# Scattering normalised rows to the experts' slots: from DRAM in the routing stage, or from SBUF in the experts' stage

## The chip, the cores and the metric

The kernel runs on one core of a Trainium2 chip as one launch. The core has a tensor engine (PE, with its weight loads shown apart as PEld), a vector engine (DVE), a scalar engine (ACT), GpSimd (POOL) and a sync engine (SP) that issues most DMAs. The metric is the device time of the launch in microseconds; a version's time is the median of its runs.

## The reference, cut to what matters

Two layers run over x of 8 batches of 256 tokens, 256 wide, each layer an attention and a feed-forward, each with a residual. The place that matters is the first layer's end and the mixture of eight experts behind it:

```python
x = x + _L0_xattn_ref(_layernorm(x, axis=-1), ctx_1024, ...)   # two attentions, then relu(x @ Wf1 + bf1) @ Wf2 + bf2
x = x + _L0_ffn_ref(_layernorm(x, axis=-1), gate_w, W1, W2, W3)

def _L0_ffn_ref(x, gate_w, W1, W2, W3):
    xf = x.reshape(-1, D)
    scores = xf @ gate_w.T
    expert_weights, expert_indices = jax.lax.top_k(scores, 2)
    expert_weights = jax.nn.softmax(expert_weights, axis=-1)
    mid = jax.nn.silu(einsum('td,ehd->teh', xf, W1)) * einsum('td,ehd->teh', xf, W3)
    out_all = jnp.einsum('teh,edh->ted', mid, W2)
    ...   # the two chosen experts' rows, weighted and summed
```

Every token needs two of the eight experts only. The kernel therefore sorts the 2 x 2048 (token, expert) pairs by expert into `xs`, a DRAM tensor of 23 tiles of 256 rows, in which each tile belongs to one expert, and computes tile by tile.

## The kernel before

The program is a chain of stages: `decoder` (both attentions), `feed_forward`, `route`, `experts`, `memory_attention`, `mixture`. Each stage is one block with a queue of instructions written out by hand for each engine; the order in a queue is the order of the code, semaphores tie the queues together, and at a block's end every engine drains its pipeline and all five meet in a barrier before the next block starts.

- `feed_forward` goes batch by batch. Its last steps normalise the result (DVE, L1542, into the ring `res_n`), turn it on PE (`turn_result`, L1451) for the gate's scores (`gates`, L1460; `logits`, L1555), and store two things from SP's queue: the result itself to `xa` (L1400) and the normalised rows to the DRAM tensor `hm` (L1403), 256 KB for each batch. SP also clears `xs` with zeros (L1393), and waits at the block's end until the stores have landed (L1408).
- `route` finds each pair's slot. SP loads `hm` back into `route_rows` (L1656, eight loads). DVE finds the top two, counts them, adds up the counts, and writes `slots` (L1748, once for each of the two choices k) and at last `tile_expert`, the expert of each tile (L1752 to L1757). POOL waits for the rows, the zeros and each choice's slots, and then issues 32 indirect DMAs (L1775), each of which writes 128 rows of 1 KB to their slots in `xs`; it waits at the end until all have landed.
- `experts` goes over the 23 tiles as a pipeline. For a tile, SP reads its expert's number from `tile_expert` and loads its rows `x_in` (L1841), its up weights `up_in` (L1844, 1792 KB) and its down weights `down_in` (L1836, 896 KB), all in rings of two. ACT and DVE split each into a high and a low half in 16 bits: `up_hl` HI on ACT (L1929), LO on DVE (`up_low`, L1956), seven pieces each. PE turns the rows (`turn_rows`, L1867) into `ps_x`; ACT (L1934) and DVE (L1984) split those into `x_hl`. Then PE multiplies up (`go_up`, L1880) and, two steps later in its queue, down (`go_down`, L1892). At step t PE does go_up(t+1), turn_rows(t+2), go_down(t); SP issues down_in(t+2), x_in(t+3), up_in(t+3) and stores y(t-1).

Of the kernel before, what the change touches and what calls it, by code (L numbers as in the profile page):

```python
# [14 lines left out]
P = 128  # L15
BATCHES = 8
SEQ = 256
TOKENS = BATCHES * SEQ
D = 256
# [1305 lines left out]
def feed_forward(nc, c, rows, x, w1_hl, b1, w2_hl, b2, gain, shift, gate, out, out_normed, logits, xs, zeroed):  # L1325


    with ExitStack() as ctx:
# [28 lines left out]
        res_n = ring(sb, "res_n", [P, TT, D])  # L1357
# [19 lines left out]
        res_stored, res_n_stored = ring(sem, "res_stored"), ring(sem, "res_n_stored")  # L1377
# [4 lines left out]
        with nc.Block() as block:  # L1382
            @block.sync
            def _(sp):
# [5 lines left out]
                def step(t):  # L1390
                    old, older = t.plus(-2), t.plus(-4)
# [13 lines left out]
                pipeline(sp, step, 0, 4)  # L1405
                for k in range(2):
                    sp.wait_ge(res_stored[k], 16 * (BATCHES // 2))
                    sp.wait_ge(res_n_stored[k], 16 * (BATCHES // 2))  # L1408

            @block.tensor  # L1410
            def _(pe):
# [33 lines left out]
                def turn_result(t):  # L1445
# [3 lines left out]
                    for k in range(TT):  # L1449
                        for dc in range(DC):  # L1450
                            mm = nc.tensor.transpose(ps_r[:, dc, k * P:(k + 1) * P], res_n[t.slot][:, k, dc * P:(dc + 1) * P], c.ident[:, :])  # L1451
# [58 lines left out]
            def _(dve):  # L1510
# [10 lines left out]
                def step(t):  # L1521
# [94 lines left out]
def route(nc, c, logits, normed, xs, weights, slots, tile_expert, zeroed):  # L1616
# [6 lines left out]
    with ExitStack() as ctx:  # L1623
# [21 lines left out]
        rows = sb("rows", [P, NT, D])  # L1645
# [4 lines left out]
        gap_done, slots_done, rows_loaded, scattered = sem("gap_done"), sem("slots_done"), sem("rows_loaded"), sem("scattered")  # L1650

        with nc.Block() as block:
            @block.sync
            def _(sp):
                for b in range(BATCHES):
                    sp.dma_start(rows[:, b * TT:(b + 1) * TT, :], normed[b]).then_inc(rows_loaded, 16)  # L1656

# [102 lines left out]
            def _(pool):  # L1760
# [9 lines left out]
                pool.wait_ge(rows_loaded, 16 * BATCHES)  # L1770
                pool.wait_ge(zeroed, 16 * BATCHES)
# [697 lines left out]
```

## Time and profile before

| | us |
|---|---|
| median of 3 runs | 1415.44 (1414.83 to 1420.32) |
| the profiled execution, its own time | 1417.55 |
| its span in the trace | 1415.8 |
| feed_forward's end and route, up to tile_expert | about 500 to 524.2 in the span |
| the scatter and its end | 523.0 to 567.7 |
| the head of experts, up to the first go_up | 567.7 to 585.6 |
| the 23 tiles of experts | 585.6 to about 957 |

The profile is of one execution. Times in its rows are from the start of the span. A timeline row is the start, the duration, the engine, the line of the kernel, the operation, output and inputs, and in brackets how long the engine was idle before and what released it. PEclk is the clock that PE was granted, as a share of 2.4 GHz (0.50 is 1.2 GHz). DMA is the mean busy share of the core's 16 DMA engines.

### The profile page before, as it was taken

How to read it: one execution, taken by the hardware profiler on the slowest of the kernel's cores; microseconds unless marked ns; L12 is line 12 of the kernel's file. 1: busy time of each engine (PE TensorE's matmuls, PEld its weight loads, DVE VectorE, ACT ScalarE, POOL GpSimd, SP SyncE). 2: the span in 40 equal slices, each digit the busy share in tenths (PEclk: the TensorE clock that was granted, in tenths of full speed). 3: DMA queues.
4: the chain of work that ended last, by engine and by line, in shares of the span. 5: the costliest groups of instructions: out<-in, count | busy, mean ns of one | idle time of the engine just before them, and what ended most of it. 6: DMA issues, size and time to landing. Idle time of an engine off the chain costs nothing. (4 is left out here: it accounts for less than half of the span.)

```text
span 1415.8 us, 26094 instructions
## 1 busy us (share of the span) xinstructions
PE 1086.1 (77%) x9362; PEld 734.0 (52%) x9362; DVE 944.0 (67%) x2608; ACT 610.6 (43%) x1227; POOL 431.5 (30%) x595
## 2 busy tenths in 40 slices
PE   2788888888399820388999999991577874999998
PEld 1465544444178720277778777881234432554554
DVE  4748777776247640478888888871677752677676
ACT  2346666666255300455666666641266661000000
POOL 4235764333426637012211121116543100010010
PEclk9978889998699955699999999995599996999999
DMA  6423335231123232656666666515332211000000
GB/s 182 125 83 106 99 95 158 80 91 46 34 78 119 103 108 100 231 206 231 243 218 208 236 241 222 199 44 170 103 90 75 80 38 61 31 30 23 31 8 16
DMA packets 127397, 164.26 MB, mean 116 GB/s; under 512 B 13075, under 2 KB 106022, under 8 KB 124326
## 3 DMA queue, kind: packets, MB, share of 16 engines
q1 hardware_dynamic: 123686, 153.41, 33.2%
q0 software_dynamic: 3584, 9.18, 2.0%
q8 instruction: 76, 1.25, 0.4%
q14 instruction: 51, 0.42, 0.1%
HBM read 117.01 MB, written 45.35 MB: 115 GB/s over the span
## 5 line engine op out<-in xcount | busy, mean ns | idle before, releaser
L1880 PE MATMUL moe_ps_u<-moe_x_hl,moe_up_hl 128*128 128x256 f16 x1932 | 227.5, 277 | 41.4 <-DVE moe_up_hl L1956 33.2
L1880 PEld LDWEIGHTS moe_ps_u<-moe_x_hl,moe_up_hl 128*128 128x128 f16 x1932 | 185.3, 99 | 83.6 <-DVE moe_up_hl L1956 39.7
L2129 PE MATMUL mix_ps_e<-wr_hl,mix_u_hl 128*128 128x512 f16 x768 | 173.4, 382 | 0.0
L2006 POOL CAST moe_mid_hl<-moe_mid 128x256 f16<-128x256 f32 x161 | 68.5, 425 | 315.5 <-DVE moe_mid L1971 315.5
L547 ACT ACTIVATE dec_probs<-dec_ps_t 128x768 f32<-128x768 f32 (+1 forms) x128 | 117.2, 916 | 77.5 <-PE dec_ps_t L449 76.5
L1956 DVE SCALAR_TENSOR_TENSOR moe_up_hl<-moe_up_in,moe_up_hl 128x512 f16<-128x512 f32 x161 | 105.2, 687 | 55.9 <-ACT moe_up_hl L1929 55.9
L2241 DVE SCALAR_TENSOR_TENSOR mix_acc<-mix_ps_e,mix_shares,mix_acc 128x256 f32<-128x256 f32 x256 | 110.4, 478 | 39.7 <-PE mix_ps_e L2129 39.3
L1929 ACT ACTIVATE moe_up_hl<-moe_up_in 128x512 f16<-128x512 f32 x161 | 99.1, 619 | 63.5 <-DMA moe_up_in<-in_moe_w 63.5
L2129 PEld LDWEIGHTS mix_ps_e<-wr_hl,mix_u_hl 128*128 128x128 f16 x768 | 75.1, 98 | 84.1 <-issue 2.4
L645 DVE CUSTOM_DVE_ANT_0 dec_dropped<-dec_ps_s,mask_row 128x128 bf16<-128x128 f32 (+1 forms) x256 | 76.1, 353 | 49.8 <-PE dec_ps_s L436 49.3
L1892 PE MATMUL moe_ps_y<-moe_down_hl,moe_mid_hl 128*128 128x256 f16 x966 | 109.0, 273 | 0.0
L649 DVE TENSOR_REDUCE dec_neg_m<-dec_ps_s 128x2 f32<-128x512 f32 x128 | 82.5, 687 | 36.1 <-PE dec_ps_s L436 36.1
L1971 DVE SCALAR_TENSOR_TENSOR moe_mid<-moe_ps_u,moe_mid 128x256 f32<-128x256 f32 x161 | 66.9, 415 | 52.5 <-ACT moe_mid L1924 52.4
L1892 PEld LDWEIGHTS moe_ps_y<-moe_down_hl,moe_mid_hl 128*128 128x128 f16 x966 | 94.6, 98 | 10.7
L1197 DVE TENSOR_REDUCE mem_neg_m<-mem_ps_s 128x2 f32<-128x512 f32 x128 | 82.3, 685 | 26.5 <-PE mem_ps_s L1041 25.8
L436 PE MATMUL dec_ps_s<-dec_k_st,dec_q_st 48*128 48x256 f16 (+1 forms) x512 | 53.7, 291 | 55.4 <-DMA dec_k_st<-dec_k_dram 36.0
L1963 DVE TENSOR_TENSOR moe_mid_hl<-moe_mid,moe_mid_hl 128x256 f16<-128x256 f32 x161 | 92.1, 583 | 0.0
L1924 ACT ACTIVATE moe_mid<-moe_ps_u 128x256 f32<-128x256 f32 x161 | 61.7, 383 | 66.3 <-PE moe_ps_u L1880 59.4
L1125 ACT ACTIVATE mem_probs<-mem_ps_t 128x1024 f32<-128x1024 f32 x64 | 65.4, 1024 | 39.3 <-PE mem_ps_t L1052 39.1
L481 PE MATMUL dec_ps_far<-dec_probs,dec_v 128*32 128x256 f32 (+1 forms) x1024 | 68.9, 391 | 2.4 <-DVE dec_att L658 1.1
L436 PEld LDWEIGHTS dec_ps_s<-dec_k_st,dec_q_st 48*128 48x128 f16 x512 | 17.3, 97 | 94.7 <-DMA dec_k_st<-dec_k_dram 40.0
L1974 DVE SCALAR_TENSOR_TENSOR moe_down_hl<-moe_down_in,moe_down_hl 128x256 f16<-128x256 f32 x161 | 66.2, 411 | 0.0
(275 smaller groups left out, 1965.6 us busy)
## 6 DMA issues: line engine op xcount, KB each, us to landing
moe_up_in<-in_moe_w SPq DMA_DIRECT2D x23, 1792.0 KB, 7.5
moe_down_in<-in_moe_w SPq DMA_DIRECT2D x23, 896.0 KB, 4.6
dec_q_dram<-dec_q_hl SPq DMA_DIRECT2D x48, 128.0 KB, 1.9
dec_k_dram<-dec_k_hl SPq DMA_DIRECT2D x48, 128.0 KB, 1.9
dec_q_st<-dec_q_dram SPq DMA_DIRECT2D x64, 96.0 KB, 2.6
dec_k_st<-dec_k_dram SPq DMA_DIRECT2D x64, 96.0 KB, 2.7
xs<-zeros SPq DMA_DIRECT2D x8, 736.0 KB
moe_x_in<-xs SPq DMA_DIRECT2D x23, 256.0 KB, 4.3
```

The source lines that it names most:

```text
L436: return nc.tensor.matmul(ps_s[h % 2][:, k, 0:keys_of(n, k)], q_st[n % 2][at:at + STACK, pair, k * P:(k + 1) * P], k_st[n % 2][at:at + STA ...
L547: nc.scalar.activation(probs[p % 4][:, :, 0:w], ps_t[p % 2][:, :, 0:w], ACT.Exp, scale=SCALE).then_inc(exps_done, 1)
L645: ins = nc.vector.tensor_tensor_reduce(dropped[h % 2][:, k, 0:w], ps_s[h % 2][:, k, 0:w], c.mask_row[:, SEQ - w:SEQ], -1.0, -MASKED, ALU.a ...
L649: nc.vector.tensor_reduce(neg_m[n % 2][:, :, column(h):column(h) + 1], ps_s[h % 2][:, :, :], AX.X, ALU.max, negate=True).then_inc(max_done, 1)
L1197: nc.vector.tensor_reduce(neg_m[n % 2][:, :, column(h):column(h) + 1], ps_s[h % 2][:, :, :], AX.X, ALU.max, negate=True).then_inc(max_done, 1)
L1880: mm = nc.tensor.matmul(bank[:, m, :], up_hl[t.slot][:, w, m, dc, f * P:(f + 1) * P], x_hl[t.slot][:, x, dc, :], start=(dc == 0 and w == x ...
L1892: mm = nc.tensor.matmul(ps_y[t.slot][:, k, :], mid_hl[t.slot][:, m, f, k * P:(k + 1) * P], down_hl[t.slot][:, w, f, :], start=(f == 0 and ...
L1929: nc.scalar.activation(up_hl[new.slot][:, HI, :, :, f * P:(f + 1) * P].rearrange("p m c h -> p (m c) h"), up_in[new.slot][:, :, :, f * P:( ...
L1956: nc.vector.scalar_tensor_tensor(up_hl[t.slot][:, LO, :, :, at].rearrange("p m c h -> p (m c) h"), up_in[t.slot][:, :, :, at].rearrange("p ...
L1963: nc.vector.tensor_tensor(mid_hl[t.slot][:, LO, f, :], mid[:, f, :], mid_hl[t.slot][:, HI, f, :], ALU.subtract).then_inc(mid_split, 1)
L2129: mm = nc.tensor.matmul(ps_e[fill % RING][:, :, :], u_hl[t.slot][:, r, dc, k * P:(k + 1) * P], wr_hl[:, m, dc, 2 * q:2 * q + 2, :], start= ...
L2241: nc.vector.scalar_tensor_tensor(acc[t.slot][:, k, :], ps_e[(TT * q + k) % RING][:, j, :], shares[t.slot][:, k, 2 * q + j:2 * q + j + 1], ...
```

## The change

The normalised rows get an SBUF tensor of their own for all batches, `normed_rows`, which lives until the end. `feed_forward` writes them there and turns them from there; the ring `res_n`, the tensor `hm`, its eight stores and its eight loads are gone, and so are DVE's two waits before a slot of `res_n` is written again. The 32 indirect DMAs and their wait for the zeros move from POOL's queue in `route` to the head of POOL's queue in `experts`; nothing in `route` waits for them. In `experts` SP issues the first tile's up and down weights and the second's up weights, and only then waits for the scatter and loads the first tile's rows. Of the later tiles SP loads the rows right behind the down weights, one step later than before. For the first tile DVE does all seven `up_low` ahead of the low half of the rows.

```diff
@@ feed_forward
-        res_n = ring(sb, "res_n", [P, TT, D])
@@ sync
-                    if older.within():
-                        sp.wait_ge(res_n_done, TT * (older.n + 1))
-                        sp.dma_start(out_normed[older.n], res_n[older.slot][:, :, :]).then_inc(res_n_stored[older.slot], 16)
@@ vector
-                        if d.before(2):
-                            dve.wait_ge(res_n_stored[d.slot], 16 * d.turn)
-                            dve.wait_ge(r_turned, d.n - 1)
                         for k in range(TT):
-                            nc.vector.tensor_scalar(res_n[d.slot][:, k, :], res[d.slot][:, k, :], mv_o[d.slot][:, k, 0:1],
+                            nc.vector.tensor_scalar(normed_rows[:, d.n * TT + k, :], res[d.slot][:, k, :], mv_o[d.slot][:, k, 0:1],
@@ route
-            @block.sync
-            def _(sp):
-                for b in range(BATCHES):
-                    sp.dma_start(rows[:, b * TT:(b + 1) * TT, :], normed[b]).then_inc(rows_loaded, 16)
@@ gpsimd
-                pool.wait_ge(rows_loaded, 16 * BATCHES)
-                pool.wait_ge(zeroed, 16 * BATCHES)
-                for k in range(2):
-                    pool.wait_ge(slots_done, k + 1)
-                    for t in range(NT):
-                        nc.gpsimd.indirect_dma_start(xs[:, :], bass.IndirectOffsetOnAxis(ap=slots[:, k, t:t + 1], axis=0),
-                                                     rows[:, t, :], None).then_inc(scattered, 16)
-                pool.wait_ge(scattered, 16 * 2 * NT)
@@ experts, sync
+                def load_rows(t):
+                    if t.n == 0:
+                        sp.wait_ge(scattered, 16 * 2 * NT)
+                    if t.before(2):
+                        sp.wait_ge(turned, t.n - 1)
+                    sp.dma_start(x_in[t.slot][:, :, :], xs_t[t.n]).then_inc(x_loaded[t.slot], 16)
+
                 def step(t):
                     new, ahead, old = t.plus(2), t.plus(3), t.plus(-1)
+                    if t.n == -1:
+                        load_rows(t.plus(1))
                     if new.within():
 ...
                         sp.dma_start(down_in[new.slot][:, :, :], w2[e]).then_inc(down_loaded[new.slot], 16)
+                    if new.within() and new.n > 0:
+                        load_rows(new)
                     if ahead.within():
                         e = sp.value_load(tile_expert[0:1, bass.ds(ahead.n, 1)], min_val=0, max_val=E - 1)
-                        if ahead.before(2):
-                            sp.wait_ge(turned, ahead.n - 1)
-                        sp.dma_start(x_in[ahead.slot][:, :, :], xs_t[ahead.n]).then_inc(x_loaded[ahead.slot], 16)
@@ vector
+                    if new.n == 0:
+                        for f in range(0, HC, 2):
+                            up_low(new, f)
                     if new.within():
                         dve.wait_ge(x_hi, new.n + 1)
 ...
                     for f in range(0, HC, 2):
-                        if new.within():
+                        if new.within() and new.n > 0:
                             up_low(new, f)
@@ gpsimd
+                pool.wait_ge(zeroed, 16 * BATCHES)
+                for k in range(2):
+                    for t in range(NT):
+                        nc.gpsimd.indirect_dma_start(xs[:, :], bass.IndirectOffsetOnAxis(ap=slots[:, k, t:t + 1], axis=0),
+                                                     rows[:, t, :], None).then_inc(scattered, 16)
```

POOL's queue from the end of `route` to the first tile of `experts`, before; an unconditional branch is the end of a block or the start of the next, and `barrier` stands for the meeting of the five engines:

```order
L1768 AFFINE_SELECT route_triangle<-route_triangle 128x128 [waits route_made]
L1775 DMA xs<-route_rows,slots 5888x256 [waits route_slots_done,zeroed,route_rows_loaded]
L1775 DMA xs<-route_rows,slots 5888x256 x15
L1775 DMA xs<-route_rows,slots 5888x256 [waits route_slots_done]
L1775 DMA xs<-route_rows,slots 5888x256 x15
L1652 UNCONDITIONAL_BRANCH [waits route_scattered]
L1998 UNCONDITIONAL_BRANCH [waits barrier_Pool_Activation_PE_DVE_SP_gather]
L2006 CAST moe_mid_hl0<-moe_mid 128x256 [waits moe_mid_done] x7
```

Here all 32 indirect DMAs and the wait for their landing are behind `slots` and ahead of the barrier. The same place on POOL now:

```order
L1754 AFFINE_SELECT route_triangle<-route_triangle 128x128 [waits route_made]
L1643 UNCONDITIONAL_BRANCH
L1989 UNCONDITIONAL_BRANCH [waits barrier_Pool_Activation_PE_DVE_SP_gather]
L1994 DMA xs<-normed_rows,slots 5888x256 [waits zeroed]
L1994 DMA xs<-normed_rows,slots 5888x256 x31
L2003 CAST moe_mid_hl0<-moe_mid 128x256 [waits moe_mid_done] x7
```

The scatter has gone from ahead of the barrier to behind it, and the wait for its landing has left POOL.

SP's queue at the head of `experts`, before (0 and 1 behind a name are the slots of a ring):

```order
L1828 UNCONDITIONAL_BRANCH [waits barrier_Pool_Activation_PE_DVE_SP_release]
L1838 TENSOR_LOAD tile_expert
L1838 ISA x2
L1841 DMA moe_x_in0<-xs 128x2x256
L1844 ISA
L1844 DMA moe_up_in0<-in_moe_w13 128x3584
L1833 TENSOR_LOAD tile_expert
L1833 ISA x2
L1836 ISA
L1836 DMA moe_down_in0<-in_moe_w2 128x1792
```

Here the first tile's rows are the first DMA behind the barrier. SP's queue now, from the first load of weights on:

```order
L1832 DMA moe_up_in0<-in_moe_w13 128x3584
L1822 TENSOR_LOAD tile_expert
L1822 ISA x2
L1825 ISA
L1825 DMA moe_down_in0<-in_moe_w2 128x1792
L1829 TENSOR_LOAD tile_expert
L1829 ISA x2
L1832 ISA
L1832 DMA moe_up_in1<-in_moe_w13 128x3584
L1815 DMA moe_x_in0<-xs 128x2x256 [waits moe_scattered]
```

The first tile's rows, which stood first, now stand behind three loads of weights, with the wait for the scatter; the second tile's down weights, its rows and the third tile's up weights follow.

DVE's queue at the head of `experts`, before (`up_hl` are the halves of the up weights, `x_hl` those of the rows):

```order
L1951 UNCONDITIONAL_BRANCH [waits barrier_Pool_Activation_PE_DVE_SP_release]
L1956 SCALAR_TENSOR_TENSOR moe_up_hl0<-moe_up_in0,moe_up_hl0 128x4x128 [waits moe_up_hi] x3
L1984 TENSOR_TENSOR moe_x_hl0<-moe_ps_x,moe_x_hl0 128x512 [waits moe_x_hi]
L1956 SCALAR_TENSOR_TENSOR moe_up_hl0<-moe_up_in0,moe_up_hl0 128x4x128 [waits moe_up_hi] x4
L1971 SCALAR_TENSOR_TENSOR moe_mid<-moe_ps_u0,moe_mid 128x256 [waits moe_silu_done]
```

Here the rows' low half stands between three and four pieces of the weights. The same place on DVE now:

```order
L1939 UNCONDITIONAL_BRANCH [waits barrier_Pool_Activation_PE_DVE_SP_release]
L1944 SCALAR_TENSOR_TENSOR moe_up_hl0<-moe_up_in0,moe_up_hl0 128x4x128 [waits moe_up_hi] x7
L1975 TENSOR_TENSOR moe_x_hl0<-moe_ps_x,moe_x_hl0 128x512 [waits moe_x_hi]
L1959 SCALAR_TENSOR_TENSOR moe_mid<-moe_ps_u0,moe_mid 128x256 [waits moe_silu_done]
L1962 SCALAR_TENSOR_TENSOR moe_down_hl0<-moe_down_in0,moe_down_hl0 128x256 [waits moe_down_hi]
```

All seven pieces of the first tile's weights now stand ahead of the rows; of later tiles nothing moved on DVE.

## Rows read from the trace of the kernel before

**Rows 1.** Stretches: busy us of PE, PEld, DVE, ACT, POOL; PEclk; DMA; GB/s.

```profile
524.50:568.70 44.20, 0.00 (x0) 0.00 (x0) 0.00 (x0) 0.00 (x0) 29.76 (x31) 0.50 0.23 95
568.70:585.60 16.90, 1.11 (x4) 0.71 (x4) 5.17 (x8) 4.22 (x8) 0.00 (x0) 0.50 0.93 366
```

**Rows 2.** Timeline of the scatter: its first, second and last indirect DMA.

```profile
522.93 0.41 DVE L1752 TENSOR_TENSOR route_ended<-route_ends,route_tile_numbers 1x184 f32<-1x184 f32 x1
522.97 1.24 POOL L1775 DMA_INDIRECT xs<-route_rows,slots  x1 [11.17 <-DVE slots L1748]
...
524.52 0.96 POOL L1775 DMA_INDIRECT xs<-route_rows,slots  x1 [0.30 <-issue]
...
562.46 0.96 POOL L1775 DMA_INDIRECT xs<-route_rows,slots  x1 [0.30 <-issue]
```

**Rows 3.** The end of route's block: duration ns min/median/max, first and last start.

```profile
L1652 DVEq DRAIN  x1: 448/448/448, 523.8 to 523.8; - x1
...
L1652 POOLq COMPARE_BRANCH  x1: 33/33/33, 564.9 to 564.9; - x1
L1652 POOLq DRAIN  x1: 2675/2675/2675, 565.0 to 565.0; - x1
```

**Rows 4.** Tensor xs, 522 to 568: issue to landing of the scatter's DMAs.

```profile
DMA to landing us min/median/max: 2.4/2.4/2.7
```

**Rows 5.** Timeline of the head of experts.

```profile
568.75 0.37 SPq L1841 DMA_DIRECT2D moe_x_in<-xs  x1
...
571.40 1.11 PE L1867 MATMUL moe_ps_x<-ident,moe_x_in 128*128 128x128 f32 x4 [54.66 <-DMA moe_x_in<-xs]
...
581.86 0.56 ACT L1934 CAST moe_x_hl<-moe_ps_x 128x512 f16<-128x512 f32 x1
582.46 0.69 DVE L1984 TENSOR_TENSOR moe_x_hl<-moe_ps_x,moe_x_hl 128x512 f16<-128x512 f32 x1 [0.30 <-ACT moe_x_hl L1934]
...
585.61 12.53 PE L1880 MATMUL moe_ps_u<-moe_x_hl,moe_up_hl 128*128 128x256 f16 x84 [13.10 <-DVE moe_up_hl L1956]
```

**Rows 6.** A later block's start: POOL's barrier event, then POOL's first gather.

```profile
L98 POOLq EVENT_SEMAPHORE  x4: 17/17/17, 378.3 to 960.2; - x4
...
961.05 1.01 POOL L1292 DMA_INDIRECT mem_y<-ys,slots  x1 [12.29 <-POOLq L98]
```

**Rows 7.** Stretch with eight gathers beside loads from SP, columns as rows 1.

```profile
962.00:970.00 8.00, 0.00 (x0) 0.00 (x0) 0.00 (x0) 0.00 (x0) 5.87 (x8) 0.50 1.06 359
```

**Rows 8.** An indirect DMA beside DVE (timeline); the head's `up_low` (groups by line).

```profile
995.01 0.73 DVE L1245 TENSOR_SCALAR mem_h_rows<-mem_sums,mem_mv,mem_rstd 128x256 f32<-128x256 f32 x2
995.18 1.12 POOL L1277 DMA_INDIRECT mem_kv_rows<-table,mem_best_row  x1 [5.95 <-DVE mem_best_row L1217]
...
L1956 DVE SCALAR_TENSOR_TENSOR moe_up_hl<-moe_up_in,moe_up_hl 128x512 f16<-128x512 f32 x7 | 4.6, 687 | 55.9 <-ACT moe_up_hl L1929 55.9
```

**Rows 9.** DMA issues on the page: count, KB each, us to landing.

```profile
moe_up_in<-in_moe_w SPq DMA_DIRECT2D x23, 1792.0 KB, 7.5
moe_down_in<-in_moe_w SPq DMA_DIRECT2D x23, 896.0 KB, 4.6
```

**Rows 10.** Waits of SP, then of POOL, and feed_forward's last drain on PE.

```profile
SPq L1408 <- DMA hm<-ff_res_n: 3.6, 1, 3.6
...
POOL xs L1775 <- DVE slots L1748: 11.2, 1, 11.2
...
L1382 PEldq DRAIN  x1: 1902/1902/1902, 508.4 to 508.4; - x1
```

**Rows 11.** Steady state of experts: a tile; landing of down_in, then of x_in.

```profile
871.21 0.34 SPq L1836 DMA_DIRECT2D moe_down_in<-in_moe_w  x1
...
884.81 0.60 PE L1867 MATMUL moe_ps_x<-ident,moe_x_in 128*128 128x128 f32 x4
...
DMA to landing us min/median/max: 4.4/4.6/14.1
...
DMA to landing us min/median/max: 2.6/4.3/13.7
```

More of the change, by code:

```diff
@@ L1322, in _, with feed_forward @@
                         add_outputs(mixed)
-def feed_forward(nc, c, rows, x, w1_hl, b1, w2_hl, b2, gain, shift, gate, out, out_normed, logits, xs, zeroed):
+def feed_forward(nc, c, rows, x, w1_hl, b1, w2_hl, b2, gain, shift, gate, out, normed_rows, logits, xs, zeroed):
     with ExitStack() as ctx:
@@ L1390, in step @@
                 def step(t):
-                    old, older = t.plus(-2), t.plus(-4)
+                    old = t.plus(-2)
                     if t.within():
@@ L1400, in step @@
                         sp.dma_start(out[old.n], res[old.slot][:, :, :]).then_inc(res_stored[old.slot], 16)
-                    if older.within():
-                        sp.wait_ge(res_n_done, TT * (older.n + 1))
-                        sp.dma_start(out_normed[older.n], res_n[older.slot][:, :, :]).then_inc(res_n_stored[older.slot], 16)
-                pipeline(sp, step, 0, 4)
+                pipeline(sp, step, 0, 2)
                 for k in range(2):
                     sp.wait_ge(res_stored[k], 16 * (BATCHES // 2))
-                    sp.wait_ge(res_n_stored[k], 16 * (BATCHES // 2))
             @block.tensor
@@ L1613, in _, with route @@
                 pipeline(pool, step, 1, 2)
-def route(nc, c, logits, normed, xs, weights, slots, tile_expert, zeroed):
+def route(nc, c, logits, weights, slots, tile_expert):
     with ExitStack() as ctx:
@@ L1644, in route @@
         gap, exped, both = sb("gap", [P, NT]), sb("exped", [P, NT]), sb("both", [P, NT])
-        rows = sb("rows", [P, NT, D])
         ps_p = ctx.enter_context(nc.psum_tensor("route_ps_p", [P, BANK], F32))
@@ L1769, in _, with experts @@
                                         pattern=[[1, P]], channel_multiplier=-1).then_inc(made, 1)
-                pool.wait_ge(rows_loaded, 16 * BATCHES)
-                pool.wait_ge(zeroed, 16 * BATCHES)
-                for k in range(2):
-                    pool.wait_ge(slots_done, k + 1)
-                    for t in range(NT):
-                        nc.gpsimd.indirect_dma_start(xs[:, :], bass.IndirectOffsetOnAxis(ap=slots[:, k, t:t + 1], axis=0),
-                                                     rows[:, t, :], None).then_inc(scattered, 16)
-                pool.wait_ge(scattered, 16 * 2 * NT)
-def experts(nc, c, xs, w13, w2, tile_expert, ys, matrices):
+def experts(nc, c, rows, slots, xs, zeroed, w13, w2, tile_expert, ys, matrices):
     with ExitStack() as ctx:
@@ L1800, in experts @@
         E, HC = w2.shape[0], w2.shape[2]
+        NT = slots.shape[2]
         x_in, x_hl = ring(sb, "x_in", [P, TT, D]), ring(sb, "x_hl", [P, 2, DC, SEQ], F16)
@@ L1808, in experts @@
         ps_y = ring(ps, "ps_y", [P, TT, D])
+        scattered = sem("scattered")
         x_loaded, up_loaded, down_loaded = ring(sem, "x_loaded"), ring(sem, "up_loaded"), ring(sem, "down_loaded")
@@ L2379, in program @@
         ctx_hl = dram("ctx_hl", [2, D, TOKENS], F16)
-        xa, hm = dram("xa", rows), dram("hm", rows)
+        xa = dram("xa", rows)
+        normed_rows = sb("normed_rows", [P, BATCHES * TT, D])
         logits = sb("logits", [P, BATCHES * TT, E])
@@ L2393, in program @@
             feed_forward(nc, c, resident, i["x"], w1_hl, i["bf1"], w2_hl, i["L0_xattn_bf2"], i["L0_xattn_g3"], i["L0_xattn_be3"],
-                         i["gate"], xa, hm, logits, xs, zeroed)
-        route(nc, c, logits, hm, xs, shares, slots, tile_expert, zeroed)
+                         i["gate"], xa, normed_rows, logits, xs, zeroed)
+        route(nc, c, logits, shares, slots, tile_expert)
         wc_hl, ws_hl, cent_hl = parts(ctx, "wc_hl", [D]), parts(ctx, "ws_hl", [D]), parts(ctx, "cent_hl", [routed])
         wr_hl = parts(ctx, "wr_hl", [routed, D])
-        experts(nc, c, xs, i["moe_w13"], i["moe_w2"], tile_expert, ys,
+        experts(nc, c, normed_rows, slots, xs, zeroed, i["moe_w13"], i["moe_w2"], tile_expert, ys,
                 [([i["mem_wc"]], flat(wc_hl)), ([i["centroids"]], flat(cent_hl)), ([i["mix_ws"][0], i["mix_ws"][1]], flat(ws_hl)),
```

6 lines of the change are left out of this document (3 added, 3 removed).

## The prediction, made before the result

> **What bounds the kernel now.** I read the page's forty slices first. PE's digits fall to 0 in one place only, a good third of the way in; that is the place of the change, and the busy shares of the whole span say nothing about it. The stretches cut at that place show why [rows 1]: from 524.5 to 568.7 no engine but POOL works, and the DMA engines are 23% busy at 95 GB/s; from 568.7 to 585.6 the opposite, POOL idle and the DMA engines 93% busy at 366 GB/s. Two pieces of work that use different things stand one behind the other.
>
> The timeline gives the chain through that gap. The scatter's first indirect DMA starts at 522.97 and its last at 562.46 [rows 2]; from the second on they follow every (562.46 - 524.52) / 30 = 1.265 us, 0.96 of work and 0.30 of issue. Each lands 2.4 after its start [rows 4]. The view of the block's end then tells what a look at the timeline alone would hide: POOL's wait for the landings is over at 564.9, but its drain takes another 2.68, to 567.7, and only then does the barrier open [rows 3]. SP reads the expert's number and issues the first tile's rows at 568.75; PE turns them from 571.40; and the first `go_up` starts at 585.61, released by DVE's last piece of the up weights [rows 5]. So the end of the gap hangs on weights that were asked for only after the scatter had ended. From 585.61 the 23 tiles run, and everything later hangs on them: what moves that start moves the end by as much.
>
> **The change part by part.** The sum is the time of the first `go_up`, against the profiled execution (1417.55, span 1415.8).
>
> *Stores and loads of the normalised rows: 0.* The eight stores: SP waits 3.6 for the last of them at the block's end, but PE's drain there, from 508.4 for 1.90, ends at 510.3, after it [rows 10]. If PE were quicker, the cover would be gone and up to 3.6 could be won; it isn't. The eight loads: what released POOL's first scatter was DVE's `slots`, after a wait of 11.2 [rows 10]; the rows were there. In SP's queue nothing on the path stood behind either. The two waits taken from DVE released nothing in the trace.
>
> *The scatter starts later: +2.2.* It now waits not for the first choice's slots but for the block's end: DVE's last drain ends at 523.8 + 0.45 = 524.25 [rows 3]. From there to POOL's first indirect DMA I take 0.95: at a later block start it came 0.85 after POOL's barrier event [rows 6], and from POOL's drain (567.7) to SP's first DMA, a register load included, it was 1.05 [rows 3, 5]. That is 525.2 against 522.97. Bounds 1.9 to 2.6.
>
> *The scatter itself: +1.7, bounds -0.3 to +4.5.* 31 steps of 1.265 are 39.2, against 39.5 before, since the first took 1.24 instead of 0.96, with DVE instructions beside it [rows 2]: -0.3. New is what runs beside it: SP's loads, and seven `up_low` of 0.687 on DVE [rows 8]. The loads I cost at nothing: eight gathers keep their step (8 starts in 8 us, 5.87 busy as far as they are counted there) while the DMA engines are saturated at 359 GB/s [rows 7]. For DVE two rows give a price: the first scatter, beside an instruction with two SBUF inputs, was 0.28 longer, and a gather beside a DVE instruction on SBUF took 1.12, 0.16 longer [rows 2, 8]. Nothing for a DVE instruction is the lower end, its whole 0.687 the upper. I take 0.28, the row with two SBUF inputs as `up_low` has them: 7 x 0.28 = 2.0; the ends are 0 and 4.8.
>
> *The end of the scatter: -3.75.* SP now waits for the landings itself, and issues the rows some 0.1 after. Before, 564.9 to 568.75 = 3.85 went to POOL's drain, the barrier and SP's register load [rows 3, 5]. All three are now over long before: POOL's drain in `route` stands behind nothing but a select, and SP has done its register loads beside the scatter.
>
> *The weights leave the path: -11.7.* From SP's issue of the rows to PE is 2.65, and from PE to `go_up` was 14.21 [rows 5]. Of that only the rows' own steps remain: 1.11 on PE, 0.56 on ACT, 0.69 on DVE, and three hand-overs of some 0.05, together 2.5 [rows 5]. What hides the rest is the scatter: up, down and the next up are 4480 KB [rows 9], at 366 GB/s [rows 1] 12.5 us from about 525; with the scatter's traffic beside them they are there by 541, and the conversions, under 5 us of ACT and DVE [rows 8], end by 546. The rows come at about 571: 25 us of cover. Without it the 11.7 would be back on the path. All seven `up_low` being ahead of the rows' low half in DVE's queue matters here; before, four of them stood behind it.
>
> *SP's queue behind the new wait.* The second tile's down weights, its rows and the third tile's up weights stand behind it. They are issued by about 570, where before they went at 573 to 586; who waits for them is ACT and PE some 12 us after `go_up` begins, against landings of 4.3 to 7.5 [rows 9, 11]: 0. POOL is free again at 568, before the first cast is asked for.
>
> *Rows of later tiles one step later: 0.* In the steady state x_in now goes right behind down_in, issued at 871.21, and PE turns those rows at 884.81 [rows 11]: with 0.4 for the issue, 13.2 of slack against a median landing of 4.3.
>
> Sum: +2.2 - 0.3 + 2.0 - 3.75 - 11.7 = -11.5. The profiled execution would take 1406.0; it was 2.1 above the median, and the median would be 1415.4 - 11.5 = **1403.9**. With DVE's price at 0 it is 1401.9, at its upper end 1406.7; a first x_in that lands at its median instead of 2.65 adds 1.7.
>
> PE's clock enters on neither side: it is at its lower level all through the gap [rows 1] and will be at the new start.
>
> **A port that is locked (rival 1).** Every `up_low` could hold POOL's descriptor work for its whole length, 7 x 0.687 = 4.8 instead of 2.0: 1406.7. Against it: the first scatter overlapped three DVE instructions and lost 0.28 in all. The Trainium skill says so much (SBUF — State Buffer, section SBUF: two separate sides): DVE and GpSimd share a pair of ports, which the first comer holds for its whole instruction; a DVE instruction with two SBUF inputs shuts out a GpSimd instruction that reads SBUF. By that rule this rival is the time; the trace bears out a delay, but no full one.
>
> **Loads that push the scatter out (rival 2).** If POOL could not write descriptors while the weights' 12.5 us of transfer fill the queues, the scatter would lose that much: 1403.9 + 12.5 = 1416.4 at the most, no change. Against it stand the eight gathers at full step [rows 7], though they are gathers, and eight.
>
> **Rows that come too late (rival 3, slower).** If x_in behind down_in in every tile took longer than its slack of 13.2, PE would wait in each of 21 tiles. The point from which it makes the kernel slower is 13.2 + 11.5 / 21 = 13.75. At down_in's longest landing, 14.1 [rows 11], it costs 21 x 0.9 = 18.9: 1422.8. For it: x_in's longest landing is 13.7, and down_in now stands ahead of it. Against: the median is 4.3, and up_in goes out 3 us after it, as before.
>
> **Not beside (rival 4).** If the weights were held with the scatter all the same, only the drain and the barrier would be saved, and the start lost: 1415.4 + 2.2 - 3.75 = 1413.9. SP's order, three loads ahead of the wait, speaks against it.
>
> **How the numbers follow.** Forecast 0.76, rival 1 0.09, rival 2 0.07, rival 3 0.04, rival 4 0.04. Half a per cent is 7.1 us, about what a measurement of this kernel can tell from no change: below 1408.4 is faster, and that holds the forecast and rival 1, 0.85; rivals 2 and 4 are the same, 0.11; rival 3 slower, 0.04. The range goes from 1400 (no price on DVE, and the shortest ends of the start) to 1409 (rival 1 with a slow first x_in); rivals 2 to 4, 0.15, are left out.
>
> **What would show it.** Right: weights of the first tile issued at about 525, before most of the scatter; indirect DMAs starting near 525.2 in steps of 1.265, a few longer where `up_low` runs; x_in of the first tile issued 2.5 after the last start, near 569; `go_up` near 574 with the rows' low half as its releaser, no longer `up_low`. Steps that stay long in the whole first 15 us would mean rival 2, PE waiting for x_in in later tiles rival 3. The forecast is wrong if the scatter takes over 46 us.

## The result, and the profile after

| | before | after |
|---|---|---|
| median, us (runs) | 1415.52 (7) | 1403.40 (7) |
| lowest to highest, us | 1407.11 to 1420.32 | 1400.95 to 1408.88 |
| profiled execution, us | 1417.55 | 1402.28 |
| its span, us | 1415.8 | 1400.5 |

The medians are 12.1 us apart. The ratio of the two kernels over their runs is 0.9921, with a 95% interval of 0.9894 to 0.9947: the change is faster, by 7.5 to 15 us as far as the whole time can tell. The prediction was 1403.9 us, in a range of 1400 to 1409.

The gap in which POOL worked alone is still there, but the weights are now inside it. Three stretches of that gap in the changed kernel show this (busy us of PE, PEld, DVE, ACT, POOL; the granted clock; DMA share; GB/s):

```profile
520.00:530.00 10.00, 0.00 (x0) 0.00 (x0) 1.31 (x6) 0.00 (x0) 5.95 (x6) 0.50 0.62 221
530.00:541.00 11.00, 0.00 (x0) 0.00 (x0) 4.50 (x7) 3.75 (x7) 8.56 (x9) 0.50 0.89 368
541.00:565.00 24.00, 0.00 (x0) 0.00 (x0) 0.00 (x0) 0.00 (x0) 17.75 (x19) 0.50 0.29 103
```

In [rows 1] one stretch had 95 GB/s and a busy POOL, the next 366 GB/s and an idle POOL. Now 530 to 541 has 368 GB/s, a busy POOL, and DVE's and ACT's work on the first weights. PE's clock is at its lower level in all of them, as before. The timeline of the changed kernel gives the head of the new stage:

```profile
519.52 0.17 DVE L1734 CAST slots<-route_slot 128x16 int32<-128x16 f32 x1
...
521.32 0.16 DVE L1743 TENSOR_SCALAR tile_expert<-route_owner 1x23 int32<-1x23 f32 x1
522.52 1.24 POOL L1994 DMA_INDIRECT xs<-normed_rows,slots  x1 [13.08 <-POOLq L1643]
522.75 0.36 SPq L1832 DMA_DIRECT2D moe_up_in<-in_moe_w  x1
523.91 0.35 SPq L1825 DMA_DIRECT2D moe_down_in<-in_moe_w  x1
...
525.04 0.34 SPq L1832 DMA_DIRECT2D moe_up_in<-in_moe_w  x1
```

The scatter now starts 3.00 us behind the first `slots` (it was 1.10), released by the barrier of line 1643; SP's three weight loads go out between its first steps. The end of the scatter, and the way to the first `go_up`, in the same timeline:

```profile
563.27 0.96 POOL L1994 DMA_INDIRECT xs<-normed_rows,slots  x1 [0.30 <-issue]
565.70 0.39 SPq L1815 DMA_DIRECT2D moe_x_in<-xs  x1
...
568.41 0.34 SPq L1832 DMA_DIRECT2D moe_up_in<-in_moe_w  x1
...
568.50 1.11 PE L1855 MATMUL moe_ps_x<-ident,moe_x_in 128*128 128x128 f32 x4 [54.12 <-DMA moe_x_in<-xs]
569.65 0.59 ACT L1922 CAST moe_x_hl<-moe_ps_x 128x512 f16<-128x512 f32 x1 [35.41 <-PE moe_ps_x L1855]
570.27 0.69 DVE L1975 TENSOR_TENSOR moe_x_hl<-moe_ps_x,moe_x_hl 128x512 f16<-128x512 f32 x1 [33.42 <-ACT moe_x_hl L1922]
...
571.11 1.22 PE L1868 MATMUL moe_ps_u<-moe_x_hl,moe_up_hl 128*128 128x256 f16 x5 [1.49 <-DVE moe_x_hl L1975]
```

Against [rows 5], `go_up` is now released by the rows' low half, and no longer by the weights'. From the last indirect DMA to x_in it takes 2.43, in place of 6.29.

All kernels below are compared by the same five times, each between two marks of a profiled execution: the decoder's end (POOL's event of line 98, [rows 6]), the first `slots`, the first `go_up`, and the experts' end (the second such event). "Way" is from `slots` to `go_up`, the stretch the prediction was about.

| kernel | decoder | to `slots` | way | tiles | the rest | span |
|---|---|---|---|---|---|---|
| before | 378.3 | 143.6 | 63.74 | 374.6 | 455.6 | 1415.8 |
| after | 375.7 | 143.8 | 51.59 | 373.7 | 455.7 | 1400.5 |
| e1_rows_only | 376.2 | 143.8 | 62.07 | 373.7 | 462.0 | 1417.8 |
| e2_head_no_overlap | 377.4 | 145.2 | 60.44 | 374.5 | 459.2 | 1416.7 |
| e3_rows_by_dram | 373.8 | 143.6 | 51.51 | 373.6 | 454.9 | 1397.4 |
| e4_low_halves_behind | 379.8 | 143.5 | 52.88 | 374.6 | 460.0 | 1410.8 |
| e5a_two_inputs | 373.7 | 142.4 | 50.26 | 374.4 | 457.1 | 1397.9 |
| e5b_one_input | 382.9 | 145.9 | 50.43 | 374.4 | 462.9 | 1416.5 |
| e6_after_again | 378.8 | 144.2 | 51.57 | 373.6 | 458.4 | 1406.6 |
| e7_second_tile_too | 380.0 | 143.5 | 51.05 | 369.9 | 458.9 | 1403.3 |

The way is 12.15 us shorter after the change, and repeats there: 51.59, 51.57 and, with the rows sent through DRAM, 51.51. The kernel before was profiled once, and e1 and e2 show below that 1.4 to 1.7 of its 63.74 are a slow landing of the first weights. The decoder runs the same code in all ten and still takes 373.7 to 382.9; the rest takes 454.9 to 462.9. So of the 15.3 us between the two profiled spans, 2.6 in the decoder are not the change's. The part on PE's clock, at the end of the experiments, says what goes with these two columns.

### The profile page after: what moved, and what is told of

It reads as the page before. It is cut to its first block and busy times, and to the rows that moved or that the text cites. A ratio compares the mean times of both kernels' runs of the same rounds, so it can differ in the third digit from the quotient of the medians.

```text
span 1400.5 us, 26069 instructions
## 1 busy us (share of the span) xinstructions
PE 1075.2 (77%) x9362; PEld 730.0 (52%) x9362; DVE 942.8 (67%) x2608; ACT 611.0 (44%) x1227; POOL 432.3 (31%) x595
## 3 DMA queue, kind: packets, MB, share of 16 engines
HBM read 114.91 MB, written 43.25 MB: 113 GB/s over the span
```

## Experiments

**Which part of the change brings the time?** Theory A: the overlap of scatter and weight loads, and the drain of POOL that leaves the path. Rival B: less traffic, since the rows stay in SBUF.

**e1_rows_only**, rows kept, scatter left in `route` (against the kernel before):

```diff
-                        sp.wait_ge(res_n_done, TT * (older.n + 1))
-                        sp.dma_start(out_normed[older.n], res_n[older.slot][:, :, :]).then_inc(res_n_stored[older.slot], 16)
...
-                            nc.vector.tensor_scalar(res_n[d.slot][:, k, :], res[d.slot][:, k, :], mv_o[d.slot][:, k, 0:1],
+                            nc.vector.tensor_scalar(normed_rows[:, d.n * TT + k, :], res[d.slot][:, k, :], mv_o[d.slot][:, k, 0:1],
...
-                for b in range(BATCHES):
-                    sp.dma_start(rows[:, b * TT:(b + 1) * TT, :], normed[b]).then_inc(rows_loaded, 16)
...
-                pool.wait_ge(rows_loaded, 16 * BATCHES)
```

> The kernel before with one part of the change: the normalised rows stay in SBUF (eight stores, eight loads and their waits are gone), and the scatter stays at the end of the route, with the barrier behind it. Theory A (the gain is the overlap of scatter and weight loads): the stores and loads were hidden, so the time is that of the kernel before, 1415.5 us within 1.5 us, and from the scatter's last DMA_INDIRECT to the first go_up matmul it stays near 21.5 us. Rival B (the gain is the 2.1 MB less written and 2.1 MB less read): near 1403.4 us.

Measured: 1418.97 us, ratio 1.0032 (1.0010 to 1.0055) to the kernel before. No gain; B falls. The timeline of e1_rows_only shows the path of before:

```profile
521.08 1.24 POOL L1760 DMA_INDIRECT xs<-normed_rows,slots  x1 [11.15 <-DVE slots L1734]
...
521.85 0.43 DVE L1743 TENSOR_SCALAR tile_expert<-route_owner 1x23 int32<-1x23 f32 x1
...
560.56 0.96 POOL L1760 DMA_INDIRECT xs<-normed_rows,slots  x1 [0.30 <-issue]
566.89 0.37 SPq L1826 DMA_DIRECT2D moe_x_in<-xs  x1
567.48 0.36 SPq L1829 DMA_DIRECT2D moe_up_in<-in_moe_w  x1
...
574.66 3.75 ACT L1914 ACTIVATE moe_up_hl<-moe_up_in 128x512 f16<-128x512 f32 x7 [61.88 <-DMA moe_up_in<-in_moe_w]
...
582.07 1.67 PE L1865 MATMUL moe_ps_u<-moe_x_hl,moe_up_hl 128*128 128x256 f16 x7 [11.35 <-DVE moe_up_hl L1941]
```

From the last indirect DMA to x_in again 6.33, and `go_up` waits for the weights. The way is 62.07; the 1.7 us against 63.74 lie in the first up weights, which came 7.2 after their issue here (567.48 to 574.66) and 8.9 after it in the profile of before:

```profile
569.34 0.36 SPq L1844 DMA_DIRECT2D moe_up_in<-in_moe_w  x1
...
578.21 3.75 ACT L1929 ACTIVATE moe_up_hl<-moe_up_in 128x512 f16<-128x512 f32 x7 [63.55 <-DMA moe_up_in<-in_moe_w]
```

That the median is 4 us above before (1414.77 in the 28 runs beside it) was not expected: 1.5 us was the bound. In this profile it stands neither in the way nor in the tiles but in the rest, 462.0. About half of it goes with PE's granted clock, averaged over each run: the runs of before are 3.8 us shorter for each 0.01 more of it (a straight line through the 28, correlation -0.71), and e1's ten were granted 0.8847 on average, against 0.8905. Where the other 2 us come from is not shown.

**e2_head_no_overlap**, the scatter in its new place, SP's and DVE's order of before (against the changed kernel; SP's part, DVE's is the edit of e4 below):

```diff
-                    if t.n == -1:
-                        load_rows(t.plus(1))
...
-                    if new.within() and new.n > 0:
-                        load_rows(new)
...
+                        if ahead.n == 0:
+                            sp.wait_ge(scattered, 16 * 2 * NT)
+                        if ahead.before(2):
+                            sp.wait_ge(turned, ahead.n - 1)
+                        sp.dma_start(x_in[ahead.slot][:, :, :], xs_t[ahead.n]).then_inc(x_loaded[ahead.slot], 16)
```

> The changed kernel, but SyncE's and VectorE's order in the experts' stage is that of the kernel before: the scatter stands at the head of the experts' stage, x_in of tile 0 with its wait for the scatter is SyncE's first transfer, and all weights are issued behind it. Theory A: the scatter starts 1.9 us later, the drain of GpSimd and the barrier behind it go (3.75 us), and the weights stay on the path: near 1413.6 us, so a sixth of the gain. Rival B (the place of the scatter alone, or the residence of the rows, brings it): near 1403.4 us.

Measured: 1414.97 us, ratio 1.0001 (0.9979 to 1.0022). No gain that can be told from none, and far from 1403.4: the new place alone does not do it. The timeline of e2_head_no_overlap has both small terms:

```profile
522.56 0.17 DVE L1734 CAST slots<-route_slot 128x16 int32<-128x16 f32 x1
...
525.56 1.24 POOL L1985 DMA_INDIRECT xs<-normed_rows,slots  x1 [13.08 <-POOLq L1643]
...
565.14 0.96 POOL L1985 DMA_INDIRECT xs<-normed_rows,slots  x1 [0.31 <-issue]
567.57 0.37 SPq L1823 DMA_DIRECT2D moe_x_in<-xs  x1
```

The start is 3.00 behind `slots` (1.9 later than before), x_in 2.43 behind the last indirect DMA (3.86 earlier), together -2.0; the way fell to 60.44, of which 1.4 is again the weights' quicker landing. From 60.44 to 51.59 only the order of SP and DVE differs: 8.9 us are what this order brings in this pair of profiles, what the scatter loses beside DVE already taken off.

**e3_rows_by_dram**, the overlap with the rows sent through DRAM as before (against the changed kernel; the eight stores and the ring `res_n`, not shown here, are back as well):

```diff
+                for b in range(BATCHES):
+                    sp.dma_start(rows[:, b * TT:(b + 1) * TT, :], normed[b]).then_inc(rows_loaded, 16)
...
+                pool.wait_ge(rows_loaded, 16 * BATCHES)
                 pool.wait_ge(zeroed, 16 * BATCHES)
```

> The changed kernel, but with the rows sent through DRAM again (eight stores in the feed-forward, eight loads in the route into the same SBUF tensor, the scatter waits for them too); the overlap of scatter and weight loads stays. Theory A: same time as the changed kernel, 1403.4 us within 1.5 us, since stores and loads lie beside other work. Rival B (residence): near 1415.5 us. Between the two ends the distance from 1403.4 us is what the residence itself is worth.

Measured: 1400.61 us, ratio 0.9913 (0.9880 to 0.9946), the same as the changed kernel within the intervals (2.8 us below it, where 1.5 was expected), at 117.01 MB read in place of 114.91. The way is 51.51 and the stretch to `slots` 143.6, in place of 51.59 and 143.8. So between these marks the residence is worth nothing in time, and the medians, which can tell these two kernels apart to some 6 us, show nothing either; A stands. (What the residence gives is less DRAM traffic, and it takes SBUF.)

**Do the low halves' places matter? e4_low_halves_behind** (against the changed kernel):

```diff
-                    if new.n == 0:
-                        for f in range(0, HC, 2):
-                            up_low(new, f)
...
-                        if new.within() and new.n > 0:
+                        if new.within():
                             up_low(new, f)
```

> The changed kernel, but with VectorE's order of the kernel before at the first tile: three of the seven low halves of the up weights ahead of the rows' low half, four behind it. Theory A: four low halves of 0.62 us come back onto the path, 2.5 us, less some 0.5 us since four fewer VectorE instructions run beside the scatter and fewer DMA_INDIRECT are stretched: 1405.4 us, the first go_up matmul 2.0 us later after the slots than in the changed kernel. Rival C (the low halves never mattered, since matmuls of the first columns start before they end): 1403.4 us or a little less.

The timeline of e4_low_halves_behind:

```profile
573.66 2.49 DVE L1944 SCALAR_TENSOR_TENSOR moe_up_hl<-moe_up_in,moe_up_hl 128x512 f16<-128x512 f32 x4
...
576.20 0.39 PE L1868 MATMUL moe_ps_u<-moe_x_hl,moe_up_hl 128*128 128x256 f16 x1 [3.81 <-DVE moe_up_hl L1944]
```

The four come back with 2.49 us of work, `go_up` waits for them, and it starts 2.3 later behind the rows' low half. The scatter lost 0.9 less (39.85 from first to last, after the change 40.75), so the way is 1.3 longer, not 2.0; rival C falls. The median, 1408.42 (ratio 0.9963, 0.9933 to 0.9993), is 5.0 above 1403.4, more than the way explains; its profile is 4.1 longer in the decoder and 4.3 in the rest, which the edit does not touch.

**What does an indirect DMA lose beside DVE?** The prediction had a price of 0.28 for each `up_low`. The changed kernel's timeline, where the two meet:

```profile
531.66 0.96 POOL L1994 DMA_INDIRECT xs<-normed_rows,slots  x1 [0.30 <-issue]
531.67 0.71 DVE L1944 SCALAR_TENSOR_TENSOR moe_up_hl<-moe_up_in,moe_up_hl 128x512 f16<-128x512 f32 x1 [10.19 <-ACT moe_up_hl L1917]
532.71 0.69 DVE L1944 SCALAR_TENSOR_TENSOR moe_up_hl<-moe_up_in,moe_up_hl 128x512 f16<-128x512 f32 x1 [0.33 <-ACT moe_up_hl L1917]
532.93 1.31 POOL L1994 DMA_INDIRECT xs<-normed_rows,slots  x1 [0.30 <-issue]
533.75 3.10 DVE L1944 SCALAR_TENSOR_TENSOR moe_up_hl<-moe_up_in,moe_up_hl 128x512 f16<-128x512 f32 x5 [0.35 <-ACT moe_up_hl L1917]
534.54 1.34 POOL L1994 DMA_INDIRECT xs<-normed_rows,slots  x1 [0.30 <-issue]
536.18 1.50 POOL L1994 DMA_INDIRECT xs<-normed_rows,slots  x1 [0.30 <-issue]
```

Besides the first of all, three of the 32 are longer, by 0.35, 0.38 and 0.54: 1.27 in all. The one at 532.93 started 0.22 into an `up_low` that ends at 532.71 + 0.69 = 533.40, which is 0.12 + 0.35 behind its start. The same 0.12 fits the other two: 534.54 + 0.12 + 0.38 = 535.04 is the end of the second of the five (0.69 long, (3.10 - 0.69) / 4 = 0.60 apart), and 536.18 + 0.12 + 0.54 = 536.84 that of the last, 536.85. The one at 531.66 started 0.01 ahead of an `up_low` and lost nothing; that `up_low` was 0.02 longer. This reads as: 0.12 us after its start the DMA needs something that a running DVE instruction holds to its end. The profiles of e3, e4, e6 and e7 have ten more such meetings with an `up_low`, with losses from 0.08 to 0.54, and in each the start, 0.12 and the loss add up to an `up_low`'s end within 0.01. To test the reading, **e5a_two_inputs** and **e5b_one_input** put more DVE instructions beside the scatter:

```diff
                     at = slice(f * P, (f + 1) * P)
+                    if t.n == 0:
+                        for j in range(2):
+                            nc.vector.scalar_tensor_tensor(spare[:, 2 * f + j, :, :], up_in[0][:, :, :, at].rearrange("p m c h -> p (m c) h"),
+                                                           LIFT, up_hl[0][:, HI, :, :, at].rearrange("p m c h -> p (m c) h"),
+                                                           ALU.mult, ALU.subtract)
```

> The changed kernel with 14 more VectorE instructions beside the scatter, two ahead of each of the first tile's seven low halves, of the same operation and size (128x512, both inputs in SBUF); their result goes to a spare buffer, added work whose output nobody reads. It asks what a DMA_INDIRECT (0.96 us, one each 1.265 us) loses beside VectorE. Theory A (it is held from its first tenth of a microsecond until the VectorE instruction then running ends, and gets in before the next one): some 13 us of VectorE meet 8 DMA_INDIRECT, each 0.15 to 0.55 us longer, none over 1.6 us; from the first to the last DMA_INDIRECT 42 to 43 us, in place of 40.75 in the changed kernel. Rival B (a row of such instructions keeps it out to the row's end): one DMA_INDIRECT of several microseconds, and over 45 us. Rival C (the pacing is the DMA engines', VectorE has no part): three stretched ones as before, 40.75 us.

All three forecasts were wrong: 21 DVE instructions in a row, 13.4 us, and not one indirect DMA beside them was longer than 0.96. From first to last it took 39.49, as if DVE were idle, and the way was 50.26, 1.3 shorter than in the changed kernel (the one execution took 1399.62 us). The timeline of e5a_two_inputs shows why:

```profile
528.21 1.36 DVE L1947 SCALAR_TENSOR_TENSOR moe_spare<-moe_up_in,moe_up_hl 128x512 f16<-128x512 f32 x2 [10.14 <-ACT moe_up_hl L1918]
528.24 0.96 POOL L2000 DMA_INDIRECT xs<-normed_rows,slots  x1 [0.30 <-issue]
529.49 0.74 DVE L1950 SCALAR_TENSOR_TENSOR moe_up_hl<-moe_up_in,moe_up_hl 128x512 f16<-128x512 f32 x1
529.51 0.96 POOL L2000 DMA_INDIRECT xs<-normed_rows,slots  x1 [0.30 <-issue]
...
531.42 0.68 DVE L1950 SCALAR_TENSOR_TENSOR moe_up_hl<-moe_up_in,moe_up_hl 128x512 f16<-128x512 f32 x1
```

The first DMA started 0.03 behind a DVE instruction and came through; DVE paid instead (1.36 for two, 0.74 for one, where 0.68 stands elsewhere). Two such DVE instructions take 1.2 undisturbed, 1.27 or 1.28 here with what a DMA adds, and the DMA's step is 1.265: once in step they stay so, and each DMA seems to get in at a boundary between two instructions. A's mechanism is not refuted by this, but its count is: how many meetings cost something is a matter of phase, not of number. C's mechanism falls with the thirteen losses that each end with a DVE instruction.

In **e5b_one_input** the added line is a copy:

```diff
+                            nc.vector.tensor_copy(spare[:, 2 * f + j, :, :], up_in[0][:, :, :, at].rearrange("p m c h -> p (m c) h"))
```

> The same with 14 copies instead (128x512, 32-bit in, 16-bit out, one input in SBUF); the result goes to a spare buffer that nobody reads. Theory A (what holds a DMA_INDIRECT is a VectorE instruction with two inputs in SBUF): no DMA_INDIRECT that starts during a copy is longer than 0.96 us, only those that meet the seven low halves are, and from the first to the last it takes 40.5 to 41 us. Rival D (any VectorE instruction holds it): 42 to 43 us, as with two inputs.

The timeline of e5b_one_input:

```profile
540.87 0.76 DVE L1947 CAST moe_spare<-moe_up_in 128x512 f16<-128x512 f32 x2 [10.11 <-ACT moe_up_hl L1918]
540.94 1.19 POOL L1998 DMA_INDIRECT xs<-normed_rows,slots  x1 [0.30 <-issue]
541.54 0.68 DVE L1948 SCALAR_TENSOR_TENSOR moe_up_hl<-moe_up_in,moe_up_hl 128x512 f16<-128x512 f32 x1
542.14 0.76 DVE L1947 CAST moe_spare<-moe_up_in 128x512 f16<-128x512 f32 x2
```

The only long one, 1.19, started 0.07 into a copy of one input: held 0.23, to about that copy's end (two in 0.76). So two inputs are not needed, and A's condition falls; D's 42 to 43 us don't come either (39.78), since after that one meeting two copies and an `up_low` (540.87 to 542.14) again make a step of 1.27. The one execution took 1418.19 us, 18.6 more than e5a, with the same way to 0.2 us. Where a row has the start of the DVE instruction itself, a DMA that came up to 0.04 behind it passed, and one that came 0.07 or more behind it was held to that instruction's end (e3_rows_by_dram has another at 0.07, held 0.50). But inside a dense row, where an instruction's start has to be worked out, a DMA 0.02 behind one was held (536.18 above, against 533.75 + 4 x 0.60), so which of two close starts wins is not settled.

**e6_after_again**, the changed kernel without an edit, as a base for the next:

> The changed kernel once more, on the same chip as the next one: 1403.4 us within 2 us; its time from the slots to the first go_up matmul 51.6 us, whatever the stages before and behind take.

Measured: 1407.21 us against 1418.8 of before on this chip, ratio 0.9915 (0.9885 to 0.9946). The way is 51.57, as expected; the time is 3.8 above 1403.4, outside the 2 us. Both kernels read 3 to 4 us higher here than at first, their ratio does not.

**e7_second_tile_too**, a further step (against the changed kernel; `up_high` is ACT's high half, as a function):

```diff
-                    if new.within():
+                    if new.within() and new.n != 1:
                         act.wait_ge(up_loaded[new.slot], 16 * (new.turn + 1))
...
+                    if new.n == 0:
+                        nxt_up = new.plus(1)
+                        act.wait_ge(up_loaded[nxt_up.slot], 16 * (nxt_up.turn + 1))
+                        for f in range(HC):
+                            up_high(nxt_up, f)
+                        nc.scalar.activation(mid[:, 0, 0:1], c.eps[:, 0:1], ACT.Silu)
...
-                        for f in range(0, HC, 2):
-                            up_low(new, f)
+                        for n in range(2):
+                            for f in range(HC):
+                                up_low(new.plus(n), f)
```

> An attempt at a better kernel: the changed one, with the up weights of the second tile, too, split on ScalarE and VectorE beside the scatter, and ScalarE's table for Silu loaded there by one dummy instruction. Theory A: in the changed kernel the second tile's go_up waits 5.29 us for VectorE's low halves, and the table load of 1.28 us stands between the first go_up and the first Silu; some 4 to 5 us go, seven more low halves stretch the scatter by 1.3 us more: 3 us below the changed kernel, near 1400.5 us, and the second go_up matmul 13.5 to 14.5 us behind the first in place of 18.1. Rival E (what the second tile gains, the third gives back, since it then waits for its own weights): the same time as the changed kernel, or 1 us more.

Measured: 1402.77 us, ratio 0.9885 (0.9854 to 0.9915). On the same chip the means are 1402.3 (six runs) and 1406.8 (five of the changed kernel): 4.5 less, with a 95% interval of 3.5 to either side. What the second tile waited for in the changed kernel, and in e7_second_tile_too, in the timelines:

```profile
589.23 0.57 PE L1868 MATMUL moe_ps_u<-moe_x_hl,moe_up_hl 128*128 128x256 f16 x2 [5.29 <-DVE moe_up_hl L1944]
```

```profile
543.72 4.30 DVE L1954 SCALAR_TENSOR_TENSOR moe_up_hl<-moe_up_in,moe_up_hl 128x512 f16<-128x512 f32 x7 [4.17 <-ACT moe_up_hl L1899]
544.55 1.30 POOL L2005 DMA_INDIRECT xs<-normed_rows,slots  x1 [0.30 <-issue]
546.15 1.50 POOL L2005 DMA_INDIRECT xs<-normed_rows,slots  x1 [0.31 <-issue]
546.82 1.28 ACT L1929 ACT_TABLE_LOAD   x1
...
574.52 2.72 PE L1868 MATMUL moe_ps_u<-moe_x_hl,moe_up_hl 128*128 128x256 f16 x12 [1.49 <-DVE moe_x_hl L1986]
...
588.94 0.49 PE L1868 MATMUL moe_ps_u<-moe_x_hl,moe_up_hl 128*128 128x256 f16 x3 [2.34 <-issue]
```

The second `go_up` comes 14.4 behind the first, in place of 18.1, and the tiles take 369.9 in place of 373.6: the third tile gives nothing back, and rival E falls. Seven more low halves cost the scatter nothing net (40.46 from first to last): two meetings on the second tile, one on the first. Of the three kernels run several times on this chip it is the fastest.

**What goes with the decoder's time and the rest's.** The windows of e5a_two_inputs, the quickest decoder, and of e5b_one_input, the slowest (first the decoder, then 150 us from the experts' end; the granted clock stands ahead of the DMA share):

```profile
0.00:373.70 373.70, 268.46 (x2944) 164.47 (x2944) 252.01 (x909) 201.89 (x324) 172.50 (x218) 0.89 0.36 101
940.80:1090.80 150.00, 87.84 (x806) 46.21 (x808) 91.78 (x208) 66.95 (x113) 71.00 (x80) 0.73 0.36 108
```

```profile
0.00:382.90 382.90, 280.10 (x2944) 169.08 (x2944) 252.48 (x909) 202.10 (x324) 172.50 (x218) 0.85 0.34 98
953.60:1103.60 150.00, 88.34 (x775) 45.22 (x775) 89.35 (x203) 64.55 (x108) 70.74 (x79) 0.69 0.36 108
```

The same 2944 matmuls of the decoder keep PE busy 268.46 or 280.10, with 0.89 or 0.85 granted; over the ten profiles 0.85 and 0.86 go with 378.8 to 382.9 us, 0.87 to 0.91 with 373.7 to 378.3. Behind the experts' end every profile has the lower level for the first 30 us, and how much of the next 120 has the upper one differs: where the 150 us have 0.69 or 0.70 (e1, e4, e5b), the rest takes 460.0 to 462.9, where they have 0.73 to 0.77, 454.9 to 459.2. e1 and e4 are the two whose medians lie some us above what the way gives. Whether their timing brings the lower grant there, or chance, was not tried and stays open.

## Why the prediction was right, step by step

The way was predicted 11.5 us shorter and came out 12.15 shorter against the profile of before; against e1, whose first weights landed quicker, it is 10.5. The forecast's case is the one that came; no rival's time did.

- **Stores and loads, 0: right by the marks.** e1 and e3 show it from both sides: the stretch to `slots` is 143.6 before and in e3, 143.8 after and in e1. The 4 us of e1's median lie elsewhere.
- **Later start, +2.2: measured +1.9**, the lower bound. The drain was taken from [rows 3] with 0.448, but it is 0.18 in the changed kernel, and `tile_expert` ahead of it 0.16; in e1, where both run beside the scatter's first DMA as they did before, `tile_expert` takes 0.43. The hand-over to the first DMA, 0.95, was right: 1.0 from the end of the drain.
  The drains of POOL and DVE at the end of `route` in the changed kernel (duration in ns, start):

```profile
L1643 POOLq DRAIN  x1: 389/389/389, 509.1 to 509.1; - x1
...
L1643 DVEq DRAIN  x1: 179/179/179, 521.3 to 521.3; - x1
```

- **The scatter, +1.7: measured +1.26** (40.75 against 39.49 from first to last). Both parts behind it failed. The -0.3 rested on reading the first DMA's 1.24 as DVE's doing [rows 2]: it is 1.24 in every profile, with no DVE instruction beside it too, so it belongs to being the scatter's first. That took the 0.28 away from under the price as well: seven meetings at 0.28 were three at 0.35 to 0.54. The size came out near by luck, because the two errors went opposite ways.
- **SP's loads beside the scatter, 0: right.** At 368 GB/s every indirect DMA that met no DVE instruction kept 0.96 and 0.30; rival 2 is out. Their data landed later, up to 8.0 us after the start where it was 2.7 at most [rows 4], but the last ones, which count, again after 2.4.
- **End of the scatter, -3.75: measured -3.86**, and again -3.86 in e2 (6.29 to 2.43). POOL's drain in `route`, at 509.1 above, is long over and 0.39 long.
- **Weights off the path, -11.7: measured -11.6** (from PE's turn of the rows to `go_up` 2.61, before 14.21). The 14.21 came from the one profile of before with its slow landing; in e1 and e2, where the weights are on the path too, the stretch is 12.47 and 12.93, so against those the term is -9.9 to -10.3. That it agrees to 0.1 comes from the same profile of before on both sides. e2 and e4 show what it takes: SP's loads ahead of the wait, and all seven `up_low` ahead of the rows' low half.
- **First x_in: +0.15** (2.80 from issue to PE, before 2.65).
- **Queue behind the new wait, and rows one step later, 0: right.** The next loads went out by 568.41; x_in lands after 4.8 on the median and 5.6 at most, far below the 13.75 of rival 3, and the 23 tiles take 373.7, before 374.6.

The measured terms add to +1.9 + 1.26 - 3.86 - 11.6 + 0.15 = -12.15. The range has a slip that decided nothing: with no price on DVE and the shortest start its lower end is 1403.9 - 2.0 - 0.3 = 1401.6, not 1400.

Rival 1's time, 1406.7, did not come, but its mechanism did, where the prediction had said "a delay, but no full one". The rule of the Trainium skill (SBUF — State Buffer, section SBUF: two separate sides) is that a pair of ports is held by whichever of DVE and GpSimd comes first, for its whole instruction, and that a DVE instruction takes it in a two-port mode or, against one that reads SBUF, with two inputs there. The trace agrees as far as the DVE side goes: a DMA that came second waited to the very end of the DVE instruction, 0.23 to 0.54, behind the one-input copy too (which mode that copy runs in no run shows). It differs on the other side: a DMA that got through beside an `up_low` (started from 0.01 ahead of it to 0.04 behind) did not hold it for 0.96, but cost it under 0.1 (0.71, 0.74 and, in e4, 0.76 in place of 0.69). For small instructions the rule may hold on this side too: in e1 `tile_expert`, begun while the scatter's first DMA ran, took 0.43 in place of 0.16 and ended 0.04 ahead of that DMA's end. What fell was the prediction's way from rule to sum: it multiplied a price by all seven instructions, where only the DMAs that start inside one pay.

## What to carry to other kernels

Where one stretch has a busy GpSimd and idle DMA queues, and the next the reverse, the order of the issuing queue is what to change: here it was worth 9 us and the moved scatter 2, and the DRAM traffic saved gave no time that the marks show. Cost a contention by counting who starts inside whom, and for how long the rest of it lasts, rather than by a price for each instruction. And read a change of 10 us in 1400 from marks around its own place in the profile: in the changed kernel it repeated to 0.1 us, while unchanged stages moved by 9. Take the profile of before more than once as well: the only one here had 1.4 to 1.7 us of slow landing in it.

## What the runs showed of the hardware

- An indirect DMA of 128 rows starts every 1.265 us on GpSimd, with the DMA engines 23% or 89% busy, where no DVE instruction meets it; the first of the scatter takes 1.24 in place of 0.96 in all ten profiles.
- It waits for a running `up_low` to its end (13 meetings, 0.08 to 0.54 lost; one with a copy, 0.23), and an `up_low` grows by 0.02 to 0.07 beside it, small instructions by more (`tile_expert` 0.16 in the changed kernel, 0.43 beside one); in a dense row of DVE instructions the two can fall into step and lose nothing.
- GpSimd's drain at the end of a block cost 2.68 us [rows 3] right behind the scatter, after the scatter's landings had been waited for, and 0.39 in the changed kernel, where no scatter stands ahead of it. With the scatter in the next block it was 3.86 us less on the path.
- The decoder, which no edit touched, took from 373.7 to 382.9 us, with 0.85 to 0.91 of PE's clock granted.
